# A decoder of four layers on one core: maxima over the partitions moved to GpSimd, the last context layer with one pass of scores, film and filter fused, and the bias copy moved forward

## The chip, the cores and the metric

The kernel runs on 1 core of one Trainium2 chip. The metric is the time of one execution on the device, in microseconds. Three runs of the kernel before gave 4775.98, 4770.83 and 4765.56 us, a median of 4770.83.

## What is computed

The input x has the shape (4, 256, 128): 4 batches of 256 positions with 128 channels. A context of shape (4, 1601, 96) serves four attention layers. The masks are all true. Twelve sublayers follow one another, each adding to x: self-attention, context attention and a feed-forward part for each of four layers. Those that the change touches are these.

Layer 0's context attention has 8 heads of 128. In the kernel all 1024 queries attend over all 4 x 1601 = 6404 context places, with a softmax:

```python
q, k, v = x_norm @ Wq, context @ Wk, context @ Wv
p = softmax(1.5 * scale * q @ k.T)
x = x + (p @ v) @ Wout + bout
```

Layer 1's context attention has 16 heads of 8. At its end a flag tells whether any score was not a number; then the mean of the values replaces the result.

Layer 2's context sublayer takes the best places of the context, and then steers the normalised input with the attended context c, filters it along time by a long convolution done as a Fourier transform, steers again, and ends with a Gelu network:

```python
scale, shift = split(gate * (c @ W_film + b_film))
y = y * (1 + scale) + shift
```

Layer 3's context sublayer quantises its tensors to 8-bit integers and its weights to three values, and adds two attentions in sequence to the fused text, each with one head of 64 over the 1601 places of the same batch:

```python
for i in range(2):
    q = fused folded to 64 columns
    fused = fused + 0.1 * twice(softmax(q @ keys_i.T * scale) @ values_i)
```

## The kernel before

The work is cut into stages. A stage (`Core.stage`, L72) is a block with one program for each engine, and all engines meet at its end. Within it the engines wait for each other on semaphores. SP issues the transfers. Five places matter.

**The first load.** `WeightsAhead.use` (L655) for the first layer lets SP issue, after the layer's own weights, the four copies of `ContextAhead.load` (L1258 to L1263): all weights of the heads (2048 KB), the context by columns (2401.5 KB), the context by rows (2448 KB, written in runs of 96 floats, 51 on each of 128 partitions) and the output bias (64 KB). The stage ends when SP is through with issuing. The data is waited for in `fold_weights` (L1223).

**Layer 0's context attention**, `attend_all_places` (L956). A unit is one head, one half of the queries (512) and one part of the 51 context tiles (24 or 27); there are 32 units. Groups of four tiles run through a ring of 11 buffers. The loop over steps s, written out by hand for each engine, does in each step: scores of group s on TensorE (L985), two copies to the ring on ScalarE (L1079), running maxima on VectorE (L1129), and for the group nine steps earlier the subtraction of the maximum (L1110), the exponential (L1065) and one step later the product with the context rows (L1010). The maximum over the partitions is made at a unit's end: VectorE folds to 128x512 (L1135, L1137), TensorE turns four tiles (L994), VectorE reduces (L1141), TensorE spreads the four columns out again (L1000), ScalarE copies them to `L0x_spread` (L1053). `turn` comes one step behind the unit's last group, `spread_out` two, `place` three.

**Layer 1's flag** (L1629 to L1659). VectorE reduces marks to one column (L1649), GpSimd takes the maximum over the partitions (L1642), VectorE widens it (L1651).

**Layer 2's film and filter**, `layer2_context` (L3581). After `best_places` come a stage that multiplies by the text mask (with its own 1 KB copy, L3599), a norm (`normalise`), a turn (`to_columns`), `linear_rows` with `modulate` (four small VectorE steps for each of 8 tiles, L3618 to L3621), a stage with the filter (L3634 forward, L3650 copies, L3653 to L3658 the products, L3641 back), `linear_rows` with `modulate` once more, and an addition (L3669). Then a norm with its turn, `linear_columns` (L316) and a stage that applies the Gelu (L1882).

**Layer 3's two attentions.** `project_image` (L3743) makes keys and values for both. Only 64 partitions hold keys; partition 64 is set to one by GpSimd (L3791). `attend_image` (L3794) is called twice. For each of 4 batches TensorE first makes the scores by queries (8 matmuls, `scan`, L3816), of which VectorE takes maxima (L3928, L3932). TensorE turns the negated maxima to a row (L3822), which ScalarE copies to the queries' partition 64 (L3890). So the second pass of scores (L3833, 13 tiles, K=65) comes out with the maximum already subtracted. ScalarE takes the exponential straight out of PSUM (L3898), TensorE multiplies with the values (L3844). The rest is the division (L3939 to L3947). The order of TensorE is written out by hand (L3855 to L3884).

On TensorE a matmul of f32 data is two instructions in the trace, a transposition is one.

## Time and profile before

| what | value |
|---|---|
| median of three runs | 4770.83 us |
| lowest and highest | 4765.56 and 4775.98 us |
| time of the profiled execution | 4773.13 us |
| its span | 4771.4 us |
| TensorE matmuls busy | 3660.8 us (77%) |
| VectorE busy | 3005.6 us (63%) |
| ScalarE busy | 1894.5 us (40%) |
| GpSimd busy | 260.7 us (5%) |
| mean granted clock of TensorE | 0.866 |

The profile is of one execution. Times are from the start of the span. PE is TensorE's matmuls, PEld its weight loads, which lie beside them; DVE is VectorE, ACT ScalarE, POOL GpSimd, SP the engine that issues transfers. L and a number is a line of the kernel. A row of the timeline gives the start, the time, the engine, the line, output and inputs, the count of instructions merged, and in brackets the idle time before and what ended it. The granted clock is 1.00 at 2.4 GHz and 0.50 at 1.2 GHz. The columns of the other views stand with their rows below.

### The profile page before, as it was taken

To read this page: it belongs to the slowest core of one execution; us is meant where nothing else is said; L and a number is where in the kernel's file an instruction comes from. 1 tells how busy PE (TensorE), PEld (TensorE's weight loads), DVE (VectorE), ACT (ScalarE), POOL (GpSimd) and SP (SyncE) were. 2 spreads that over 40 slices of the span, in tenths; PEclk is the share of its full clock that TensorE was granted. 3 is DMA by queue.
4 is the path that set the end of the run, shared out by engine and by line. 5 is a ranking of instruction groups with operands and counts; after the bars stand their busy time and mean duration, and the time that the engine had idled before them with its cause. 6 is when DMAs were issued, how large, how long until landed. Compare 5 with 4: busy or idle time off the path is not lost. (4 is left out here: it accounts for less than half of the span.)

```text
span 4771.4 us, 54706 instructions
## 1 busy us (share of the span) xinstructions
PE 3660.8 (77%) x21928; PEld 1970.9 (41%) x21928; DVE 3005.6 (63%) x4214; ACT 1894.5 (40%) x2113; POOL 260.7 (5%) x112
## 2 busy tenths in 40 slices
PE   4699999999999955577776772666544785879669
PEld 2434444444444423233336552332222464545356
DVE  3466666666666666589885437699985446442541
ACT  1255555555555532244441332244431343331123
POOL 0000000000000000000000000144430000000000
PEclk9799999999999977799997895666656986888789
DMA  2000000000000000100002001000001000000000
GB/s 74 8 0 0 1 0 0 0 1 0 0 1 0 1 11 12 20 8 7 8 1 85 27 2 38 0 0 0 0 0 37 2 36 8 36 1 0 1 10 32
DMA packets 12879, 55.80 MB, mean 12 GB/s; under 512 B 2209, under 2 KB 2721, under 8 KB 11970
## 3 DMA queue, kind: packets, MB, share of 16 engines
q1 hardware_dynamic: 12626, 52.31, 3.7%
q8 instruction: 174, 2.85, 0.2%
q14 instruction: 79, 0.65, 0.0%
HBM read 48.50 MB, written 0.52 MB: 10 GB/s over the span
## 5 line engine op out<-in xcount | busy, mean ns | idle before, releaser
L985 PE MATMUL banks<-L0x_q_context,L0x_context 96*128 96x512 f32 (+1 forms) x1632 | 742.0, 596 | 10.0 <-ACT L0x_ring L1079 9.3
L1010 PE MATMUL banks<-L0x_ring,L0x_context_rows 128*97 128x512 f32 (+1 forms) x1632 | 737.5, 594 | 1.1 <-ACT L0x_ring L1065 1.1
L1079 ACT COPY L0x_ring<-banks 128x1024 f32<-128x1024 f32 (+1 forms) x416 | 413.4, 996 | 657.8 <-PE banks L985 657.8
L1129 DVE TENSOR_TENSOR L0x_maxima<-L0x_maxima,L0x_ring 128x1024 f32<-128x1024 f32 (+1 forms) x288 | 342.6, 1194 | 257.2 <-ACT L0x_ring L1079 256.1
L1110 DVE TENSOR_TENSOR L0x_ring<-L0x_ring,L0x_spread 128x2048 f32<-128x2048 f32 (+1 forms) x208 | 457.2, 2200 | 18.4 <-ACT L0x_spread L1053 18.4
L985 PEld LDWEIGHTS banks<-L0x_q_context,L0x_context 96*128 96x128 f32 (+1 forms) x1632 | 300.1, 188 | 396.7 <-issue 378.0
L1010 PEld LDWEIGHTS banks<-L0x_ring,L0x_context_rows 128*97 128x97 f32 (+1 forms) x1632 | 262.0, 164 | 416.8 <-issue 413.6
L1065 ACT ACTIVATE L0x_ring<-L0x_ring 128x2048 f32<-128x2048 f32 (+1 forms) x208 | 384.4, 1849 | 11.4 <-DVE L0x_ring L1110 11.3
L1485 ACT ACTIVATE L1x_probs<-banks 128x2048 f32<-128x2048 f32 (+1 forms) x112 | 196.7, 1757 | 260.3 <-PE banks L1415 218.5
L1518 DVE TENSOR_REDUCE L1x_maxima<-banks 128x3 f32<-128x1203 f32 (+1 forms) x176 | 241.5, 1372 | 91.2 <-PE banks L1384 91.2
L1384 PE MATMUL banks<-L1x_k,L1x_q 32*128 32x401 f32 x1024 | 181.3, 591 | 120.3 <-DVE L1x_maxima L1518 104.8
L1541 DVE SCALAR_TENSOR_TENSOR L1x_probs<-L1x_probs,L1x_floor 128x1024 f32<-128x1024 f32 (+1 forms) x208 | 252.1, 1216 | 13.1 <-ACT L1x_probs L1485 13.1
L3262 PE MATMUL banks<-L2x_k,L2x_q_of_head 128*128 128x512 f32 (+1 forms) x256 | 183.8, 813 | 0.0
L3367 DVE MAX8 L2x_top<-L2x_rest 128x8 f32<-128x1601 f32 x96 | 175.5, 1828 | 3.3
L1415 PE MATMUL banks<-L1x_q_shifted,L1x_k 32*128 32x256 f32 (+1 forms) x1664 | 170.5, 398 | 5.3 <-ACT L1x_probs L1485 4.0
L3372 DVE MATCH_REPLACE8 L2x_rest<-L2x_top,L2x_rest 128x1601 f32<-128x1601 f32 x96 | 173.8, 1810 | 0.0
L243 PE MATMUL banks<-identity,z_rows 128*128 128x128 f32 x104 | 26.7, 437 | 170.9 <-DVE z_rows L276 170.9
L1384 PEld LDWEIGHTS banks<-L1x_k,L1x_q 32*128 32x128 f32 x1024 | 57.9, 196 | 209.2 <-DVE L1x_maxima L1518 180.9
L3335 POOL TENSOR_TENSOR L2x_exp_all<-L2x_exp_all,L2x_exp_rest 128x1601 f32<-128x1601 f32 x31 | 110.9, 3577 | 258.3 <-ACT L2x_exp_top L3325 258.3
L1415 PEld LDWEIGHTS banks<-L1x_q_shifted,L1x_k 32*128 32x128 f32 (+1 forms) x1664 | 108.4, 185 | 37.4 <-ACT L1x_probs L1485 14.6
L1429 PE MATMUL banks<-L1x_probs,L1x_v 128*16 128x256 f32 (+1 forms) x1664 | 115.9, 387 | 5.9 <-DVE L1x_probs L1541 4.2
L316 PE MATMUL banks<-z_columns,L_weights 128*128 128x512 f32 (+1 forms) x216 | 110.8, 675 | 11.2 <-PEq L77 11.2
(899 smaller groups left out, 5512.4 us busy)
## 6 DMA issues: line engine op xcount, KB each, us to landing
L1f_expert_weights<-in_L1f_experts SPq DMA_DIRECT2D x16, 512.0 KB, 10.9
L2f_expert_weights<-in_L2f_experts SPq DMA_DIRECT2D x8, 512.0 KB, 5.0
L3a_expert_weights<-in_L3a_experts SPq DMA_DIRECT2D x8, 512.0 KB, 5.1
L3f_expert_weights<-in_L3f_experts SPq DMA_DIRECT2D x8, 512.0 KB, 5.7
L1x_k<-L1x_k_rows SPq DMA_DIRECT2D x64, 50.0 KB
L0x_context_rows<-in_context_rows SPq DMA_DIRECT2D x1, 2448.0 KB, 27.8
L0x_context<-in_context SPq DMA_DIRECT2D x1, 2401.5 KB, 19.4
L1x_context<-in_context SPq DMA_DIRECT2D x4, 600.4 KB, 5.1
```

The lines of the kernel that those rows point to most:

```text
L985: mm = pe.matmul(k.ps[0:height(j), i, :], c1[:, j * P:j * P + height(j)], q1[:, u // 2 % 2, :], start=True, stop=True)
L1010: mm = pe.matmul(k.ps[0:CW, bank, :], rows1[0:height(j), j, :], ring[0:height(j), s % RING, i, :], start=s == FIRST[u] and i == 0, stop=s ...
L1065: ins = act.activation(ring[:, s % RING, 0:len(full), :], ring[:, s % RING, 0:len(full), :], ACT.Exp)
L1079: act.copy(ring[0:r, s % RING, 2 * p:2 * p + len(pair), :], k.ps[0:r, 2 * p:2 * p + len(pair), :]).then_inc(copied, 1)
L1110: ins = dve.tensor_tensor(o, o, spread_top[:, u % 2, None, :].broadcast_to([P, len(full), 512]), ALU.add)
L1129: dve.tensor_tensor(o, before, ring[0:r, s % RING, 2 * p:2 * p + m, :], ALU.max).then_inc(maxed, 1)
L1384: mm = pe.matmul(k.ps[:, i, 0:WIDE], qT[row(h), g, b * S + it * P:b * S + (it + 1) * P], kT[row(h), b % 2, g, 400 * c:400 * c + WIDE], sta ...
L1415: mm = pe.matmul(k.ps[0:height(j), 3 + h, i * S:(i + 1) * S], kT[row(h), b % 2, g, j * P:j * P + height(j)], qs[row(h), u % 2, :], start=T ...
L1485: act.activation(probs[0:r, at % 2, 0:m, :].rearrange("p a (h q) -> p h a q", h=4), k.ps[0:r, 3:7, 0:m * S].rearrange("p h (a q) -> p h a ...
L1518: dve.tensor_reduce(mx[:, u % 2, items[0]:items[-1] + 1], k.ps[:, 0:len(items), 0:WIDE], X, ALU.max).then_inc(reduced, 1)
L1541: dve.scalar_tensor_tensor(out=o, in0=o, scalar=1.0, in1=floor[0:height(j), u % 2, :], op0=ALU.min, op1=ALU.max).then_inc(clipped, 1)
L3262: mm = pe.matmul(k.ps[:, i, 0:m], qh[:, h, b * S + it * P:b * S + (it + 1) * P], kT[:, b % 2, c:c + m], start=False, stop=True)
```

## The change

Five edits, of which the first and third are small.

1. In `ContextAhead.load` the copy of the output bias is issued second, ahead of the context by columns and by rows.
2. In `attend_all_places` the two sets of transposes, VectorE's reduction and ScalarE's copy are replaced by one `partition_all_reduce` of 128x512 on GpSimd, whose result lies on all partitions (`L0x_greatest`). It has the other sign, so the additions become subtractions. For odd units VectorE takes the maximum with the even unit's result before.
3. In layer 1 the flag is summed over the partitions by a matmul with ones in place of GpSimd's maximum.
4. In layer 2 `steer` holds mask, norm, turn, both films' matmuls and the first film in one stage, and `filter_long` the filter and the second film. The gate is multiplied to weights and biases ahead; sums and products go over wide tiles. The mask's copy goes with those of `filter_spectrum`. `gelu_columns` applies the Gelu to PSUM, in the stage of the matmuls.
5. In layer 3 `attend_image` has one pass of scores. Keys and queries lie twice, on partitions 0 to 63 and 64 to 127, and tiles of one group take them in turn. ScalarE copies the scores to a ring of three batches (the third lies in `L3x_big`), VectorE takes the maxima over tiles, GpSimd over partitions, VectorE subtracts, ScalarE takes the exponential in place. The scores run two batches ahead of the values.

The core of the diff:

```diff
 # ContextAhead.load
         sp.dma_start(self.heads[:], k.dram["L0x_heads"]).then_inc(self.here, 16)
+        sp.dma_start(self.bout[:], k.dram["L0_xattn_rows"].broadcast_to([P, P])).then_inc(self.here, 16)
         sp.dma_start(self.c1[:].rearrange("c (b n) -> c b n", b=B), k.dram["context"].rearrange("b c n -> c b n")).then_inc(self.here, 16)
         sp.dma_start(self.rows1[:, :, 0:CD], k.dram["context_rows"]).then_inc(self.here, 16)
-        sp.dma_start(self.bout[:], k.dram["L0_xattn_rows"].broadcast_to([P, P])).then_inc(self.here, 16)

 # attend_all_places
-            def turn(u):
...
-            def spread_out(u):
...
-            def place(u):
...
-            def greatest(u):
...
+                if u:
+                    dve.wait_ge(placed, u)
+                ins = dve.tensor_tensor(folded_top[:], top[:, 0, 0, :], top[:, 0, 1, :], ALU.max)
                 if u % 2:
+                    ins.then_inc(joined, 1)
+                    dve.wait_ge(joined, u // 2 + 1)
+                    ins = dve.tensor_tensor(folded_top[:], folded_top[:], greatest[:, 0, :], ALU.max)
+                ins.then_inc(folded, 1)
...
+        @block.gpsimd
+        def _(pool):
+            for u in range(UNITS):
+                pool.wait_ge(folded, u + 1)
+                if u >= 2:
+                    pool.wait_ge(shifted, LAST[u - 2] + 1)
+                    pool.wait_ge(differed, u // 2)
+                pool.partition_all_reduce(greatest[:, u % 2, :], folded_top[:], P, RMAX).then_inc(placed, 1)

 # layer1_context
+                pe.wait_ge(counted, 1)
+                pe.matmul(k.ps[:, 1, 0:1], k.ones[:], flag[:, 0:1], start=True, stop=True).then_inc(everywhere, 1)
                 pe.wait_ge(widened, 1)
...
-                pool.partition_all_reduce(flag[:, 1:2], flag[:, 0:1], P, RMAX).then_inc(everywhere, 1)
...
+                step(dve.tensor_copy(flag[:, 1:2], k.ps[:, 1, 0:1]))

 # steer: the VectorE part
+                dve.tensor_tensor(ct[:], ct[:], mask[:, :, None].broadcast_to([P, TILES, P]), ALU.mult).then_inc(masked, 1)
+                for n in names:
+                    dve.tensor_scalar(w[n], w[n], w["gate"], None, ALU.mult).then_inc(gated, 1)
+                for i, n in enumerate(names):
+                    step.start(dve.tensor_scalar(shift[:, i, :], w["b_" + n], w["gate"], None, ALU.mult))
+                step.settle()
+                step(dve.tensor_scalar(shift[:, :, 0:P], shift[:, :, 0:P], 1.0, None, ALU.add))
...
+                for p in range(4):
+                    dve.wait_ge(product, p + 1)
+                    step.start(dve.tensor_tensor(film[:, 0, 2 * p:2 * p + 2, :], k.ps[:, 2 + p, :].rearrange("p (t n) -> p t n", t=2),
+                                                 shift[:, 0, None, :].broadcast_to([P, 2, 2 * P]), ALU.add))
+                step.settle()
+                step(dve.tensor_tensor(xin[:], xin[:], film[:, 0, :, 0:P], ALU.mult))
+                dve.tensor_tensor(xin[:], xin[:], film[:, 0, :, P:2 * P], ALU.add)

 # filter_long: the VectorE part
+                for f in range(2):
+                    dve.wait_ge(spectral, f + 1)
...
+                    step.start(dve.tensor_tensor(ys[:, 0, f], real, kc, ALU.mult))
+                    step.start(dve.tensor_tensor(tmp[:, 0], imag, ks, ALU.mult))
+                    step.start(dve.tensor_tensor(ys[:, 1, f], real, ks, ALU.mult))
+                    step.start(dve.tensor_tensor(tmp[:, 1], imag, kc, ALU.mult))
+                    step.settle()
+                    step.start(dve.tensor_tensor(ys[:, 0, f], ys[:, 0, f], tmp[:, 0], ALU.subtract))
+                    step(dve.tensor_tensor(ys[:, 1, f], ys[:, 1, f], tmp[:, 1], ALU.add))
+                    dve.sem_inc(ready, 1)
...
+                for i in range(TPB):
+                    dve.wait_ge(back, i + 1)
+                    step(dve.tensor_tensor(times[:, i], times[:, i], k.ps[:, i, :].rearrange("p (b d) -> p b d", b=B), ALU.add))
+                    step(dve.tensor_tensor(times[:, i], times[:, i], scales[:, i], ALU.mult))
+                    step(dve.tensor_tensor(times[:, i], times[:, i], shifts[:, i], ALU.add))
+                    dve.tensor_tensor(outs[:, i], times[:, i], rows[:, i], ALU.add)

 # attend_image: TensorE's scores and order
+                for i, j in enumerate(groups[g]):
+                    r, t = min(P, CTX - j * P), slice(64 * (i % 2), 64 * (i % 2) + 64)
+                    mm = pe.matmul(k.ps[0:r, 2 * (n % 2) + i % 2, (i // 2) * S:(i // 2 + 1) * S], keys[t, b, j * P:j * P + r],
+                                   q1[t, b * S:(b + 1) * S], start=True, stop=True)
...
+            for b in range(B):
+                for g in range(G):
+                    if b + 2 < B:
+                        score(b + 2, g)
+                    add(b, g)
+                    if g == 1 and b:
+                        set_upright(b - 1)
 # attend_image: ScalarE's order
+            for b in range(B):
+                for g in range(G):
+                    exponentials(b, g)
+                    if b + 2 < B:
+                        take(b + 2, g)
+                keep(b)
 # attend_image: VectorE's order
+            maximum(0)
             for b in range(B):
                 if b + 1 < B:
+                    maximum(b + 1)
+                shift(b)
+                if b >= 2:
+                    finish(b - 2)
+            finish(B - 2)
             finish(B - 1)
+
+        @block.gpsimd
+        def _(pool):
+            for b in range(B):
+                pool.wait_ge(folded, b + 1)
+                if b >= 2:
+                    pool.wait_ge(shifted, G * (b - 1))
+                pool.partition_all_reduce(greatest[:, b % 2, :], folded_top[:], P, RMAX).then_inc(placed, 1)
```

## Rows read from the trace of the kernel before

**Rows 1.** The page: the span, and TensorE's busy time, share and instructions.
```profile
span 4771.4 us, 54706 instructions
PE 3660.8 (77%) x21928; PEld 1970.9 (41%) x21928; DVE 3005.6 (63%) x4214; ACT 1894.5 (40%) x2113; POOL 260.7 (5%) x112
```

**Rows 2.** Busy time in stretches: stretch, length, engines busy (instructions), granted clock, DMA share, GB/s.
```profile
300.00:1600.00 1300.00, 1300.00 (x3341) 550.99 (x3340) 879.45 (x714) 716.66 (x618) 0.00 (x0) 1.00 0.00 0
2100.00:2300.00 200.00, 153.88 (x1740) 77.27 (x1734) 181.45 (x164) 90.68 (x100) 0.00 (x0) 0.99 0.05 9
3150.00:3500.00 350.00, 218.79 (x532) 93.56 (x531) 338.65 (x340) 161.03 (x170) 147.09 (x44) 0.63 0.00 0
4271.40:4360.50 89.10, 85.36 (x300) 48.79 (x300) 22.04 (x52) 19.23 (x27) 0.00 (x0) 0.90 0.00 1
4363.00:4452.50 89.50, 86.14 (x300) 50.10 (x300) 21.79 (x51) 17.94 (x26) 0.00 (x0) 0.89 0.00 1
```

**Rows 3.** Timeline of the start, and one later issue of SP's.
```profile
14.01 0.68 SPq L1262 DMA_DIRECT2D L0x_context_rows<-in_context_rows  x1
14.73 24.20 SPq L1263 DMA_DIRECT2D L0x_output_bias<-in_L_xattn_rows  x1
39.41 1.64 DVE L181 BATCH_NORM_STATS2 norm_stats<-x_residual 128x6 f32<-128x128 f32 x8 [26.52 <-PEq L77]
...
3679.92 0.51 SPq L637 DMA_DIRECT2D L_weights<-in_L_attn_rows  x1
```

**Rows 4.** Timeline of layer 0's context attention around the end of one unit.
```profile
1037.35 0.69 DVE L1137 TENSOR_TENSOR L0x_folded_maxima<-L0x_maxima 128x512 f32<-128x512 f32 x1
...
1044.42 0.60 PE L994 MATMUL banks<-identity,L0x_folded_maxima 128*128 128x128 f32 x4
1044.86 3.60 PE L985 MATMUL banks<-L0x_q_context,L0x_context 96*128 96x512 f32 x8
...
1048.30 0.60 PE L1000 MATMUL banks<-identity,L0x_minus_max 128*128 128x128 f32 x4
...
1048.73 3.60 PE L1010 MATMUL banks<-L0x_ring,L0x_context_rows 128*97 128x512 f32 x8
...
1051.83 2.29 DVE L1110 TENSOR_TENSOR L0x_ring<-L0x_ring,L0x_spread 128x2048 f32<-128x2048 f32 x1 [1.06 <-ACT L0x_spread L1053]
```

**Rows 5.** GpSimd's reductions by line, and the timeline of the flag.
```profile
L3714 POOL PARTITION_ALL_REDUCE L3x_scales<-L3x_scales x3 | 1.1, 351 | 230.4 <-DVEq L3724 230.4
L2353 POOL PARTITION_ALL_REDUCE L3x_magnitude<-L3x_magnitude x1 | 0.5, 490 | 5.9 <-DVE L3x_magnitude L2298 5.9
...
2513.38 0.38 POOL L1642 PARTITION_ALL_REDUCE L1x_flag<-L1x_flag x1 [595.66 <-issue]
2513.79 0.69 DVE L1651 CAST L1x_probs<-L1x_flag 128x1024 int32<-128x1024 f32 x1 [5.63 <-POOL L1x_flag L1642]
```

**Rows 6.** Timeline of layer 2's film, filter and Gelu network.
```profile
3563.07 1.23 DVE L3605 TENSOR_TENSOR L2x_rows<-L2x_rows,L2x_text_bytes 128x1024 f32<-128x1024 f32 x1 [2.00 <-DMA L2x_text_bytes<-in_text_mask]
...
3590.33 9.90 PE L3634 MATMUL banks<-L2x_rows,L_weights 128*128 128x512 f32 x16 [7.21 <-PEq L77]
...
3596.91 0.69 DVE L3650 COPY L2x_spectra<-banks 128x512 f32<-128x512 f32 x1 [2.10 <-PE banks L3634]
...
3634.58 1.64 DVE L264 BATCH_NORM_STATS2 norm_stats<-L2x_rows 128x6 f32<-128x128 f32 x8 [0.30 <-PEq L77]
...
3642.10 9.62 PE L316 MATMUL banks<-z_columns,L_weights 128*128 128x512 f32 x16 [1.15 <-PEq L77]
...
3657.92 8.77 PE L357 MATMUL banks<-L_weights,L2x_hidden 128*128 128x128 f32 x64 [6.20 <-PEq L77]
```

**Rows 7.** Timeline of the first `attend_image`; then a group by line and shape, whole span.
```profile
4352.49 1.89 PE L3833 MATMUL banks<-L3x_q,L3x_k 65*128 65x256 f32 x8
...
L1415 PE MATMUL banks<-L1x_q_shifted,L1x_k 32*128 32x256 f32 x1536 | 154.0, 398 | 5.0 <-ACT L1x_probs L1485 3.8 <-ACT L1x_floor L1480 1.2
```

**Rows 8.** Group by line and shape in the first `attend_image`: busy us, mean ns, idle before.
```profile
L3898 ACT ACTIVATE L3x_probs<-banks 128x1024 f32<-128x1024 f32 x12 | 12.3, 1025 | 34.1 <-PE banks L3833 34.1
```

412 lines of the change are left out of this document (194 added, 218 removed).

## The prediction

> **What bounds the kernel now.** I read the page's share of engines first, then busy time in stretches, then for each edit the timeline of its stage. TensorE is busy 77% of the span [rows 1], but the stages have different limits. From 300 to 1600 us (layer 0's context attention) TensorE is busy for all 1300 us at a granted clock of 1.00, VectorE for 879 and ScalarE for 717: there only TensorE's work counts. Both calls of `attend_image` are TensorE's as well (85.4 of 89.1 us, 86.1 of 89.5), at a mean clock of 0.90 and 0.89 [rows 2]. At the start, in layer 1's flag and in layer 2's film the bound is a chain, and the reader is to follow hand-over after hand-over. The sum is made against the profiled execution (4773.13 us, 2.3 above the median of the runs, 4770.83). A measurement tells about 0.2%, some 10 us, from no change.
>
> **1. Bias copy second instead of last.** SP issues the context rows in 0.68 us, then holds 24.20 us in the issue of the small bias copy behind them; VectorE's first real work starts at 39.41, 0.48 us after SP is free [rows 3]. With the bias second, the big copy is SP's last, and nothing is queued behind it: four issues from 13.15, at 0.33, 0.43, 0.43 and 0.68 with gaps, end near 15.2, and the stage near 15.7. Who needs the data waits at 208 us. That a short copy passes behind large ones still in flight shows at 3679.92: the fifth issue in a row took 0.51 us [rows 3]. So it is the 6528 short runs of the rows copy, and not the number of copies, that held SP. Gain 23.5 us; bounds 0 (the big copy itself waits) and 24.
>
> **2. Layer 0's context attention.** Per unit (32 of them) TensorE loses two sets of four transposes. In place they take 1044.42 to 1044.86 and 1048.30 to 1048.73, so 0.44 + 0.43 = 0.87 us [rows 4]; 32 x 0.87 = 27.9 us, all on the bound. VectorE loses 32 reductions of 0.69 and 16 of 0.16 (24.7 us) and gains 16 maxima of 0.69 (11.0): nothing, since it is busy 68%. ScalarE loses 32 copies of 0.58: nothing, busy 55%.
> The new step is GpSimd's reduction of 128x512 over the partitions. No row has this width: 1 column took 0.35 us and 7 columns 0.49 [rows 5]. 6 columns for 0.14 us make 0.0233 each, so 0.35 + 511 x 0.0233 = 12.3 us on that slope. Bounds: 0.49 if the width costs nothing more, 512 x 0.35 = 179 if every column costs like the first. The kinds differ (maximum, sum), and GpSimd's spans are rough. I take 11, near the slope, since it is the only one there is. What covers it: the folded maxima are done at 1038.04 and the first subtraction that needs them started at 1051.83, 13.8 us later, behind a place in VectorE's order that the edit does not move [rows 4]. Behind that subtraction stands an exponential of 1.9 us, and its product comes only in TensorE's next step, 6.9 us on: by estimate a further 4.9 us of slack. Up to 18.7 us TensorE feels nothing; in units of six groups there is a step of 6.9 us more. Two places have no such cover: the last unit, where everything drains (11 against the 9 us that transposes and copy took), and the first use. At 2513.38 the first reduction in the program started 5.2 us after its input was there [rows 5], the later ones at once; that first use moves here. Together -1.5. Gain 26.4 us.
> Beside this row stands a page. The Trainium skill (GPSIMD Engine Reference, 3.2) gives 247,699 ns for GpSimd's `tensor_reduce` along the partitions at 128x2048; as an estimate from that page 62 us for 512 columns. It is another instruction than this one. By the rows the sum is the 26.4 above, by the page's rate the stage would lose 1275 us (worked out under the rivals); the row of 7 columns speaks against that rate.
>
> **3. Layer 1's flag.** VectorE waits 5.63 us for GpSimd, from 2508.16 to 2513.79 [rows 5]. A one-column product and a copy out of PSUM (0.25 + 0.15, with hand-overs 0.6) take its place; the four products now behind it are done before the mask is written (0.69). Gain 5.0 us; bounds 4.5 and 5.3.
>
> **4. Layer 2's film and filter.** Before, from the mask's wait at 3561.1 to the statistics at 3634.58: 73.5 us [rows 6]. After, on VectorE, `steer`: mask 1.23; gates and biases five times 0.35 to 0.39, 1.9; statistics to root 3.9; eight scalings 2.2; gain and shift 2.5; four additions of 128x512 at 0.72, 2.9; product and sum 2.5. That makes 17.1, with 0.7 of borders 17.8 (28.7 before). TensorE's 16 matmuls of the first film lie beside the norm, the 16 of the second as well. `filter_long`: eight matmuls, of which the first run at the low clock (6.6 us, as the second copy out of PSUM was reached at 3596.91 from 3590.33 [rows 6]), then twice six VectorE steps of 0.73, 8.8; D_skip 1.26 beside the way back; way back 3.6 after the last product; two tails of four steps, 5.8; borders 0.5. That makes 25.3 to 26.5, where 44.8 stood. The 64 small film steps of 0.29 to 0.42, the four copies out of PSUM and the stage of the last addition are gone. Gain 73.5 - 17.8 - 26.2 = 29.5 us; bounds 26 (TensorE at the low clock all along) and 32.
> Gelu out of PSUM: from 3642.10 to 3657.92 there are 9.6 us of TensorE, then a table load and a pass over 4096 columns in a stage of its own [rows 6]. Afterwards the last 128x512 Gelu (0.69) ends the stage: 9.6 + 0.7 + 0.6 = 10.9. Gain 4.9 us. The mask's 1 KB copy rides among the spectrum's, which wait for 20 us of context anyway: nothing.
>
> **5. `attend_image`, twice.** TensorE loses per batch the scan (six matmuls of 512, two of 65) and a turn. The scores (26 instructions of 256 columns at 0.216, 5.6 us; eight take 1.89 with 0.38 for the last one's end [rows 7]) go on two row tiles: four row tiles ran at 154.0/1536 = 0.100 a piece [rows 7], so I take a factor of 1.7 (bounds 1 and 2), 3.3 us. With the values (5.6) and the turn 9.2 us a batch at full clock, 18 at half. VectorE per batch: maxima 1.22, 1.22, 0.42, 0.69, 0.42; subtractions 3 x 1.22 + 0.42; finish 0.95; hand-overs 0.6: 9.6. ScalarE: 2 x (3 x 1.02 + 0.38) + 0.37 = 7.3 [rows 8]. GpSimd: 256 columns, 0.35 + 255 x 0.0233 = 6.3, or half of 11, 5.7.
> Each engine waits for the others in a fixed order, so I stepped through it. Shift of batch 0 starts at 16.0 us: query 1.7, scores and copies of two groups, maxima, reduction 5.7, second fold. From a shift to the next 12.7: subtraction 1.2, exponential 1.2, two values and two scores in turn on TensorE 5.5, copy 1.2, maxima to fold 3.6. The fourth shift comes 6.0 after the third, the end 12.3 later: 16.0 + 25.4 + 6.0 + 12.3 = 59.7 us at full clock. At half clock the same steps give 92. TensorE has more gaps than now. Where it was busy 77% of a stretch the clock was 0.99; where 63%, 0.63 [rows 2]. In the new order it is busy 64% at full clock. I take the low level for the first 30 us of a call: 69.5. Gain 178.6 - 139.0 = 39.6 us. The key memset of 10.8 us on GpSimd goes, but ended before its stage did: nothing.
>
> **Sum.** 23.5 + 26.4 + 5.0 + 29.5 + 4.9 + 39.6 = 128.9. 4773.1 - 128.9 = 4644.2, less 2.3 for the median: 4642 us.
>
> **Rivals.**
> *The clock stays low in `attend_image`.* 94 us a call in place of 69.5: 4691 us. For it: the 0.63 at a like share of TensorE [rows 2]. Against: at the low clock TensorE would itself be 83% busy, and such stretches were granted more. Chance 0.13.
> *The start gives nothing*: SP hangs in the rows copy itself, or the transfer that now runs beside layer 0 delays it. 4642 + 23.5 = 4665 us. Against: 0.68 us behind the same copies in rows 3. Chance 0.11.
> *GpSimd's reduction breaks its cover: slower.* It decides from 18.7 us for 512 columns. At 30 us a unit of seven groups stalls TensorE 11.3 and one of six 4.4: 16 x 15.7 = 251 us. `attend_image` at 15 us stands at 86 a call, 33 more: 4642 + 251 + 33 = 4926 us. It meets no change near 26 us. For it: VectorE works 68% of the time beside it, and the one slope is from 7 columns. Against: that slope gives 12.3. Chance 0.06.
> *Every column costs like the first*, 0.35 us: 179 us for 512. 16 x (160.3 + 153.4) = 5019 us in layer 0; in layer 3 four reductions of 90 and some 25 around them, 385 a call, 631 more: 10292 us. The 0.49 of 7 columns speaks against it. Chance 0.02. Between this and the forecast lies the rate that the Trainium skill (GPSIMD Engine Reference, 3.2) has for `tensor_reduce`: by its 62 us 16 x (43.3 + 36.4) = 1275 us, and at 31 us and 147 a call 155 in layer 3, an estimate from that page of 6072 us.
> *Cheaper still*: reduction of 5 us and `attend_image` at 58 to 60 us a call, 4642 - 20 - 4 = 4618 us. Chance 0.15.
> Forecast itself 0.53, for 4625 to 4660.
>
> **Numbers.** 4642 us. The range reaches over the clock and start rivals to 4700 and down to 4612; it leaves out the two slow reductions and some of the cheap end. Faster 0.91, same 0.01, slower 0.08, which is the two reductions.
>
> **What would show it.** VectorE's first statistics near 16 us; TensorE still busy all of layer 0's attention, some 27 us shorter, its reduction under 13 us and no wait of the subtractions for it over 2 us outside the first and last unit; 44 to 45 us between mask and statistics in layer 2; each `attend_image` near 70 us with the clock low only at its start. Wrong it would be if TensorE showed idle time in layer 0 once a unit, or if SP's rows issue took over 20 us.

## The result and the profile after

The changed kernel takes 4625.43 us in the median of 4 runs (4621.06 to 4626.79), where the kernel before took 4768.87 beside it. The ratio is 0.9696 with a 95% interval of 0.9679 to 0.9713. The profiled executions are 147.3 us apart (spans 4771.4 and 4624.1). The prediction was 4642 us with a range of 4612 to 4700, and faster at 0.91. It was right, with a gain some 15 us larger than forecast (143.4 us between the medians, 128.9 forecast).

The page of the changed kernel, span and engines' busy time, against [rows 1]:

```profile
span 4624.1 us, 53788 instructions
PE 3545.3 (77%) x21514; PEld 1886.8 (41%) x21514; DVE 3007.0 (65%) x4129; ACT 1899.2 (41%) x2110; POOL 390.9 (8%) x150
```

TensorE lost 115 us of work and stayed at 77% of the span. GpSimd gained 130 us of work, which the span does not show.

To see where the time went I cut each trace at nine places, always at the start of the same instruction: VectorE's first statistics, the first scores of layer 0's context attention, its last reciprocal, layer 1's flag, layer 2's mask multiplication, the product behind the Gelu, the first query product of the first attention of layer 3 and the last of its second one, and the first write of `L3x_joined`. The lengths between them, in us (each is a difference of two starts in the timelines; the gain at the flag lies in the stretch from the flag to layer 2's mask):

```
stretch                         before   after   difference
start to first statistics         39.4    16.1     23.3
to layer 0's attention           187.2   182.4      4.8
layer 0's attention             1500.1  1474.6     25.5
to layer 1's flag                781.2   782.1     -0.9
flag to layer 2's mask          1055.2  1050.6      4.6
mask to the Gelu's product        94.8    56.8     38.0
to the first attention           613.8   609.2      4.6
first attention, with turn        92.9    70.7     22.2
second attention, with turn       95.3    69.9     25.4
rest                             311.5   311.7     -0.2
```

**The start.** All four copies are issued in a row, and the stage's end follows at once (SPq is SyncE's queue; the columns are those of [rows 3]):

```profile
13.61 0.43 SPq L1239 DMA_DIRECT2D L0x_output_bias<-in_L_xattn_rows  x1
14.56 0.83 SPq L1241 DMA_DIRECT2D L0x_context_rows<-in_context_rows  x1
16.07 1.65 DVE L181 BATCH_NORM_STATS2 norm_stats<-x_residual 128x6 f32<-128x128 f32 x8 [3.09 <-PEq L77]
```

The big copy alone holds SyncE for 0.83 us, where the small one behind it had held it for 24.20 [rows 3].

**Layer 0's attention.** From 300 to 1600 us TensorE is still busy throughout; below it stand the two calls of `attend_image` (busy time in stretches, columns of [rows 2]):

```profile
300.00:1600.00 1300.00, 1300.00 (x3174) 538.68 (x3173) 889.75 (x700) 716.34 (x602) 117.84 (x29) 1.00 0.00 0
4171.50:4236.60 65.10, 49.13 (x220) 27.28 (x220) 36.07 (x53) 30.06 (x39) 7.00 (x4) 0.87 0.00 1
4239.50:4304.70 65.20, 49.37 (x220) 27.38 (x220) 36.01 (x53) 28.77 (x38) 6.97 (x4) 0.87 0.00 1
```

The timeline of a unit's end, and GpSimd's step as a group of the page:

```profile
1038.56 0.69 DVE L1113 TENSOR_TENSOR L0x_folded_maxima<-L0x_maxima 128x512 f32<-128x512 f32 x1
...
1039.34 4.35 POOL L1182 PARTITION_ALL_REDUCE L0x_greatest<-L0x_folded_maxima  x1 [37.27 <-DVE L0x_folded_maxima L1113]
1039.77 2.28 DVE L1082 TENSOR_TENSOR L0x_ring<-L0x_ring,L0x_greatest 128x2048 f32<-128x2048 f32 x1
...
1051.78 1.22 DVE L1082 TENSOR_TENSOR L0x_ring<-L0x_ring,L0x_greatest 128x1024 f32<-128x1024 f32 x1
...
L1182 POOL PARTITION_ALL_REDUCE L0x_greatest<-L0x_folded_maxima x32 | 127.1, 3973 | 1476.4 <-DVE L0x_folded_maxima L1113 759.5
```

The reduction of 128x512 takes 3.97 us in the mean. This one is over at 1043.69, 8 us before the first subtraction that needs it (1051.78). In [rows 4] that place held transposes, a reduction and a copy of three engines.

**Layer 1's flag.** The copy that widens the flag starts 0.66 us after the end of VectorE's reduction (2455.52), where it took 5.63 [rows 5]:

```profile
2455.25 0.27 DVE L1623 TENSOR_REDUCE L1x_flag<-L1x_nans 128x1 f32<-128x112 f32 x1
2455.57 0.38 PE L1612 MATMUL banks<-L1x_flag,ones 128*128 128x1 f32 x2 [2.12 <-DVE L1x_flag L1623]
...
2456.18 0.69 DVE L1626 CAST L1x_probs<-L1x_flag 128x1024 int32<-128x1024 f32 x1
```

**Layer 2.** The timeline of film, filter and Gelu, answering to [rows 6]:

```profile
3505.83 1.23 DVE L3594 TENSOR_TENSOR L2x_rows<-L2x_rows,L2x_text_bytes 128x1024 f32<-128x1024 f32 x1 [0.32 <-PEq L77]
...
3522.31 9.24 PE L3646 MATMUL banks<-L2x_rows,L_weights 128*128 128x512 f32 x16 [6.63 <-PEq L77]
3528.16 0.69 DVE L3672 TENSOR_TENSOR L2x_products<-banks,L2x_spectrum 128x512 f32<-128x512 f32 x1 [3.36 <-PE banks L3646]
...
3538.24 0.69 DVE L3685 TENSOR_TENSOR L2x_rows<-L2x_rows,banks 128x512 f32<-128x512 f32 x1 [0.86 <-PE banks L3655]
...
3544.19 1.64 DVE L264 BATCH_NORM_STATS2 norm_stats<-L2x_rows 128x6 f32<-128x128 f32 x8 [0.30 <-PEq L77]
...
3551.73 9.89 PE L3700 MATMUL banks<-z_columns,L_weights 128*128 128x512 f32 x16 [1.15 <-PEq L77]
3562.64 0.57 PE L357 MATMUL banks<-L_weights,L2x_hidden 128*128 128x128 f32 x3 [1.02 <-PEq L77]
```

From the mask's wait (3505.51, against 3561.07 before) to the statistics it is 38.7 us where it was 73.5; the 2.0 us of waiting for the mask's copy are gone, and the 0.3 that are left are the stage's border. From the first matmul to the product behind the Gelu it is 10.9 us instead of 15.8.

**Layer 3.** The second `attend_image`, its scores, GpSimd's steps and VectorE's subtractions, all from the timeline:

```profile
4239.81 3.75 PE L3900 MATMUL banks<-z_columns,L3x_both_halves 128*128 128x512 f32 x4 [1.03 <-PEq L77]
...
4251.04 1.06 POOL L4015 PARTITION_ALL_REDUCE L3x_greatest_score<-L3x_folded_top  x1 [31.45 <-DVE L3x_folded_top L3974]
...
4252.66 1.14 PE L3876 MATMUL banks<-L3x_q,L3x_k 64*128 64x256 f32 x8 [0.74 <-ACT L3x_ring L3929]
...
4255.69 4.24 DVE L3980 TENSOR_TENSOR L3x_ring<-L3x_ring,L3x_greatest_score 128x1024 f32<-128x1024 f32 x4
4255.87 1.97 POOL L4015 PARTITION_ALL_REDUCE L3x_greatest_score<-L3x_folded_top  x1 [3.76 <-DVE L3x_folded_top L3974]
...
4271.18 4.24 DVE L3980 TENSOR_TENSOR L3x_ring<-L3x_ring,L3x_greatest_score 128x1024 f32<-128x1024 f32 x4
...
4285.64 4.24 DVE L3980 TENSOR_TENSOR L3x_big<-L3x_big,L3x_greatest_score 128x1024 f32<-128x1024 f32 x4
...
4290.73 3.82 DVE L3980 TENSOR_TENSOR L3x_ring<-L3x_ring,L3x_greatest_score 128x1024 f32<-128x1024 f32 x4
```

The four subtractions start 15.5, 14.5 and 5.1 us after one another. GpSimd's maximum for batch 1 is there at 4257.84, yet the subtraction of batch 1 starts only at 4271.18: the maximum of batch 2 stands ahead of it in VectorE's order. The first subtraction is held in the same way: its maximum is there at 4252.10, and it starts at 4255.69 behind the maximum of batch 1.

### The profile page after: what moved, and what is told of

Its sections match the earlier page's. It is cut to its first block and busy times, and to the rows that moved or that the text cites. A ratio compares the mean times of both kernels' runs of the same rounds, so it can differ in the third digit from the quotient of the medians.

```text
span 4624.1 us, 53788 instructions
## 1 busy us (share of the span) xinstructions
PE 3545.3 (77%) x21514; PEld 1886.8 (41%) x21514; DVE 3007.0 (65%) x4129; ACT 1899.2 (41%) x2110; POOL 390.9 (8%) x150
## 5 line engine op out<-in xcount | busy, mean ns | idle before, releaser
L996 PE MATMUL banks<-L0x_ring,L0x_context_rows 128*97 128x512 f32 (+1 forms) x1632 | 737.1, 594 | 1.8 <-ACT L0x_ring L1040 1.8
L1082 DVE TENSOR_TENSOR L0x_ring<-L0x_ring,L0x_greatest 128x2048 f32<-128x2048 f32 (+1 forms) x208 | 458.2, 2205 | 45.9 <-ACT L0x_ring L1054 45.9
L1182 POOL PARTITION_ALL_REDUCE L0x_greatest<-L0x_folded_maxima x32 | 127.1, 3973 | 1476.4 <-DVE L0x_folded_maxima L1113 759.5
L1103 DVE TENSOR_TENSOR L0x_maxima<-L0x_ring 128x1024 f32<-128x1024 f32 x64 | 78.4, 1225 | 118.5 <-ACT L0x_ring L1054 118.5
## 6 DMA issues: line engine op xcount, KB each, us to landing
L0x_context<-in_context SPq DMA_DIRECT2D x1, 2401.5 KB, 20.6
```

Of the source, the lines that this page charges most:

```text
L996: mm = pe.matmul(k.ps[0:CW, bank, :], rows1[0:height(j), j, :], ring[0:height(j), s % RING, i, :], start=s == FIRST[u] and i == 0, stop=s ...
L1082: ins = dve.tensor_tensor(o, o, greatest[:, u % 2, None, :].broadcast_to([P, len(full), 512]), ALU.subtract)
L1103: dve.tensor_tensor(o, before, ring[0:r, s % RING, 2 * p:2 * p + m, :], ALU.max).then_inc(maxed, 1)
```

## Experiments

**One edit alone, four times.** Each kernel is the one before with a single edit. First the bias copy:

```diff
         sp.dma_start(self.heads[:], k.dram["L0x_heads"]).then_inc(self.here, 16)
+        sp.dma_start(self.bout[:], ...).then_inc(self.here, 16)
...
-        sp.dma_start(self.bout[:], ...).then_inc(self.here, 16)
```

> The kernel before with the bias copy second and nothing else. Theory A, each edit's gain is its own: VectorE's first statistics start near 16 us instead of 39.4 and the whole gets 23.3 us shorter (4745 from 4769). Theory B, the start interacts with what follows: in the changed kernel layer 0's context attention began 28.1 us earlier (195.8 against 223.9), though only 23.3 of it lie before the first statistics; the other 4.8 come from a higher granted clock between them (0.90 against 0.85 over that stretch). If that belongs to the earlier start, it is here too and the gain is about 28 us; if it varies from run to run, the stretch from the first statistics to the attention differs from 184.5 us by some other amount.

Then GpSimd's maxima in layer 0 (edit 2 whole, nothing else):

```diff
-            def turn(u):
...
+                pool.partition_all_reduce(greatest[:, u % 2, :], folded_top[:], P, RMAX).then_inc(placed, 1)
```

> The kernel before with only layer 0's maxima on GpSimd. Theory A: TensorE loses 32 x 0.87 us of transposes and the stage is 25 to 27 us shorter, as in the changed kernel (1503.2 to 1477.6 us); the whole 4743. Rival: some of the 25.5 us came from elsewhere (the earlier start, or the context rows landing at another time), and alone the stage gains under 20 us.

Then layer 2 (edit 4 whole):

```diff
+            steer(k, w, mask, ct, z0, xin, film, shift)
+            filter_long(k, w, spectrum, xin, z0, film, shift, xt)
...
+            gelu_columns(k, h, w["w1"], w["b1"])
```

> The kernel before with only layer 2's film, filter and Gelu rewritten. Theory A: from the end of the choice of places to the statistics 38.7 us instead of 73.5, and 4.9 us in the Gelu; the whole 40 us shorter, 4729. Rival: 3 to 5 us of that belong to a clock that stands high there only in the changed kernel (0.91 in its trace from 3505 to 3544 us), and alone the stretch takes 42 us or more.

Then layer 3 (edit 5 whole):

```diff
+                pool.partition_all_reduce(greatest[:, b % 2, :], folded_top[:], P, RMAX).then_inc(placed, 1)
...
-            pool.memset(keys[64:65], 1.0)
```

> The kernel before with only layer 3's attention changed. Theory A: each call takes 65.2 us against 89.1 and 89.5, the two with the turn between them 48 us shorter, the whole 4721. Rival: the clock in these calls depends on what ran before them; alone a call is 3 us or more off 65.2.

The flag (edit 3) was not run alone.

Measured, against 4775.75 us of the kernel before on the same chip: bias 4757.82 (ratio 0.9957, 0.9943 to 0.9972), reduction 4738.21 (0.992, 0.9905 to 0.9935), film 4733.11 (0.991, 0.9896 to 0.9925), attention 4725.87 (0.9893, 0.9876 to 0.9909). Each is under 2%, and no interval reaches 1. The stretches, cut at the same instructions as above:

```
                           before  bias  reduction  film   image  after
start to first statistics    39.4   16.2      39.2   39.9   39.2   16.1
to layer 0's attention      187.2  186.3     182.3  186.0  182.0  182.4
layer 0's attention        1500.1 1500.1    1474.6 1500.2 1502.9 1474.6
flag to layer 2's mask     1055.2 1062.5    1048.8 1050.7 1061.5 1050.6
mask to Gelu's product       94.8   94.7      94.7   56.6   95.1   56.8
first attention, turn        92.9   92.9      93.0   93.0   71.3   70.7
second attention, turn       95.3   95.3      95.3   95.2   70.2   69.9
```

Each edit changes its own stretch by what it changed in the full version, to within 0.6 us: in their stretches these four edits add up, and theory A holds. The whole times came within 5 us of those expected, except for the bias: 4757.8 instead of 4745. What does not belong to any edit are the second line and a part of the fourth. The stretch ahead of layer 0's attention took 187.2 us before and 182.0 with only the last layer changed, so its 4.8 us are not the earlier start's.

The flag-to-mask stretch took 1055.2, 1062.5 and 1061.5 us in three kernels that are alike there. With the reduction alone it took 1048.8, and 5 of those us have a cause. This kernel still has GpSimd's maximum at the flag:

```profile
2478.34 0.27 DVE L1626 TENSOR_REDUCE L1x_flag<-L1x_nans 128x1 f32<-128x112 f32 x1
2478.71 0.39 POOL L1619 PARTITION_ALL_REDUCE L1x_flag<-L1x_flag  x1 [593.38 <-DVE L1x_flag L1626]
2479.12 0.69 DVE L1628 CAST L1x_probs<-L1x_flag 128x1024 int32<-128x1024 f32 x1 [0.51 <-POOL L1x_flag L1619]
```

VectorE waits 0.51 us for it, where it waited 5.63 before, 5.57 with the bias alone, 5.51 with the film alone and 5.62 with the attention alone. In those four the flag's reduction is the program's first; here and in the changed kernel the first one stands in layer 0. So edit 2 by itself already removes what was forecast as edit 3's gain, and beside edit 2 the matmul of edit 3 (0.66) is worth nothing. Nor does layer 0 pay for being first: in the changed kernel the fold ends at 233.94 and the reduction starts at 234.08. Why the 5 us don't move there stays open.

The rest is spread. The rows of that stretch, for the bias alone and the reduction alone:

```profile
2486.90:3549.40 1062.50, 644.53 (x4866) 391.19 (x4866) 761.51 (x1065) 366.85 (x461) 219.13 (x72) 0.70 0.05 17
```
```profile
2478.30:3527.10 1048.80, 636.49 (x4866) 384.72 (x4866) 761.15 (x1066) 366.82 (x461) 219.04 (x72) 0.71 0.05 17
```

Of the 13.7 us between them 5.1 are the flag. VectorE's and ScalarE's busy times agree to 0.4 us. TensorE's is 8.0 us apart for the same 4866 instructions, at a granted clock of 0.70 and 0.71, so what varies besides is its clock. That, and the flag, is why the bias alone gained 17.9 us by the medians and 23.2 in its own stretch, and the reduction 37.5 and 25.5. Layer 0's attention varies as well: 1502.9 us with only the last layer changed.

**How far layer 0's reduction is covered.** The reduction of every unit is done n times, one waiting for the other:

```diff
+                for _ in range(3):
+                    step(pool.partition_all_reduce(greatest[:, u % 2, :], folded_top[:], P, RMAX))
                 pool.partition_all_reduce(greatest[:, u % 2, :], folded_top[:], P, RMAX).then_inc(placed, 1)
```

Four times:

> The changed kernel with each of layer 0's 32 reductions over the partitions done four times, one after the other (the same result is written four times). Their mean in the changed kernel is 3.97 us, so the step takes about 16 us. Theory A, the cover is 18.7 us (13.8 up to the first subtraction and 4.9 behind it): TensorE stays busy without a gap, the stage takes 1478 to 1484 us (the last unit alone pays 12 us, in full view), the whole 4636 to 4640 against 4625. Rival, the cover ends where the first subtraction used to start: from 13.8 us on each unit loses the difference, 2 us or more in each of 16 units of seven groups, 35 us or more besides the last unit's 12.

Six times (`range(5)`):

> The changed kernel with each of layer 0's reductions done six times, about 24 us. Theory A, cover 18.7 us and 6.9 more in units of six groups: 16 units lose 24 - 18.7 = 5.3 us each, 85 us, the last one 20 in full view, the stage near 1580 us. Rival, cover 13.8 us: 10 us in each of 16 units and 3 in the others, over 210 us. A third way is that the step is not six times as long because the mean of 3.97 us holds contention with VectorE, which would show in the durations first.

Ten times (`range(9)`):

> The changed kernel with each of layer 0's reductions done ten times. Four took 11.3 us together and six 15.1 us, 1.9 us for each further one, so ten take about 23 us. Theory A, the cover is 18.7 us in units of seven groups and 25.6 in units of six: 16 units lose 23 - 18.7 = 4.3 us of TensorE each, 69 us, the last unit another 17: the stage about 1560 us where it was 1474.6. Rival 1, the cover ends at 15 us, just behind what six reductions took: 8 us in 16 units and 1 in the others, over 160 us with the last. Rival 2, the cover is over 23 us: only the last unit's 17 us.

Measured: 4632.49 us with four (ratio to before 0.97, 0.9684 to 0.9716), and in one run each 4635.39 with six and 4746.58 with ten. The stage took 1479.1, 1484.0 and 1593.9 us against 1474.6. With four and six TensorE has all 1300 us of 300 to 1600 busy as before, and the rest falls to the last unit. Four took 11.3 us together, not 16, so that run can't tell a cover of 13.8 us from one of 18.7. Six took 15.1 us, not 24 (the third way of that expectation, taken up below): no stall at 15.1 refutes the cover of 13.8. Ten show where the cover ends (timeline of one unit, then TensorE's waits over the stage: us in total, times, longest):

```profile
1059.93 0.69 DVE L1117 TENSOR_TENSOR L0x_folded_maxima<-L0x_folded_maxima,L0x_greatest 128x512 f32<-128x512 f32 x1
...
1081.68 1.78 POOL L1185 PARTITION_ALL_REDUCE L0x_greatest<-L0x_folded_maxima  x1
1083.50 2.29 DVE L1082 TENSOR_TENSOR L0x_ring<-L0x_ring,L0x_greatest 128x2048 f32<-128x2048 f32 x1 [11.06 <-POOL L0x_greatest L1185]
...
1087.79 5.11 PE L996 MATMUL banks<-L0x_ring,L0x_context_rows 128*97 128x512 f32 x8 [4.18 <-ACT L0x_ring L1040]
...
PE banks L996 <- ACT L0x_ring L1040: 84.1, 18, 14.9
```

From the fold's end (1060.62) to the last reduction's (1083.46) it is 22.8 us, and TensorE waits 4.18: the cover is 18.7 us. The waits come to 84.1 us where the changed kernel has 1.8, against 86 expected. The stage lost 119: of the other 37 us 36 are TensorE's own work, since line 996 is busy 773.1 us in place of 737.1. The eight matmuls behind the stall took 5.11 us instead of 3.60, and the granted clock there was 0.69 (1087 to 1092.5 us). The stall of 4.2 us cost a further 1.5 in clock.

**What the reduction costs.** Three stages that only measure are put ahead of layer 3's attention; they add time:

```diff
+            for n in (1, 7, 64, 128, 256, 512, 1024, 2048):
+                for _ in range(2):
+                    step(pool.partition_all_reduce(target[:, 0:n], source[:, 0:n], P, RMAX))
...
+                for n in (128, 256, 512, 1024):
+                    for _ in range(2):
+                        step(pool.partition_all_reduce(target[:, 0:n], source[:, 0:n], P, RMAX))
```

> The changed kernel with three stages added ahead of layer 3's attention that do no work of the kernel's: reductions over the partitions of 1, 7, 64, 128, 256, 512, 1024 and 2048 columns, twice each, alone; then 128, 256, 512 and 1024 beside VectorE in 1024-column maxima back to back; then the same beside ScalarE in 1024-column copies. Theory A, the step costs a base and a small rate by width, and what stretched it was VectorE: from 1.06 us for 256 columns and 1.78 for 512 the rate is 2.8 ns a column and the base 0.34, so 128 columns take 0.70, 1024 take 3.2 and 2048 take 6.1; beside VectorE each waits for the maximum in progress (1.2 us), beside ScalarE nothing is added. Theory B, the first-to-last spread of 1.8 to 4.35 us belongs to the step itself (a fixed alternation or the state of its code): then it shows alone too, and ScalarE or VectorE beside it make no difference.

Measured alone, for 1, 7, 256, 512, 1024 and 2048 columns (timeline of GpSimd, one of each pair; 64 and 128 columns took 0.55 and 0.70):

```profile
4173.39 0.35 POOL L4035 PARTITION_ALL_REDUCE L3x_ring<-L3x_ring  x1 [10.33 <-DVE L3x_ring L4026]
4174.28 0.40 POOL L4035 PARTITION_ALL_REDUCE L3x_ring<-L3x_ring  x1
...
4178.11 1.06 POOL L4035 PARTITION_ALL_REDUCE L3x_ring<-L3x_ring  x1
4180.42 1.78 POOL L4035 PARTITION_ALL_REDUCE L3x_ring<-L3x_ring  x1
4184.17 3.23 POOL L4035 PARTITION_ALL_REDUCE L3x_ring<-L3x_ring  x1
4190.81 6.11 POOL L4035 PARTITION_ALL_REDUCE L3x_ring<-L3x_ring  x1
```

From 256 columns on that is 0.34 us and 2.8 ns a column. Beside ScalarE's copies the same widths took 0.70, 1.06, 1.78 and 3.22 us, no more. Beside VectorE's maxima (which read two tensors in SBUF) 128 columns took 1.57 and 1.25 us, 256 took 1.61 and 1.46, 512 took 2.18 and 1.89, 1024 took 3.33 and 4.00. Theory A holds in its widths and in naming VectorE; the addition, 0.1 to 0.9 us, is less than a whole maximum each time. VectorE pays as well, and more for a wider reduction: its maxima took 1.23 us with no reduction beside them, 1.52 beside 256 columns, 1.94 beside 512 and 2.80 beside 1024. The widest pair:

```profile
4214.34 3.33 POOL L4045 PARTITION_ALL_REDUCE L3x_ring<-L3x_ring  x1
4214.61 2.80 DVE L4052 TENSOR_TENSOR L3x_big<-L3x_big 128x1024 f32<-128x1024 f32 x1
```

The 4.35 us in layer 0 fit 1.78 of work and some 2.3 of being held off by the subtraction of 2.28 us beside it.

**GpSimd in layer 3.** Each of the four reductions of a call done three times:

```diff
+                for _ in range(2):
+                    step(pool.partition_all_reduce(greatest[:, b % 2, :], folded_top[:], P, RMAX))
```

> The changed kernel with each of layer 3's four reductions per call done three times. Theory A, GpSimd is not on the chain of attend_image: what holds VectorE's subtraction of batch b is the maximum of batch b + 1, which stands ahead of it and waits for ScalarE's copies; a call gets longer by 2 us at most, at its first batch. Rival, the reduction is on the chain of every batch: 2 x 2 us by 4 batches, 14 to 16 us a call, the whole near 4655 us.

Measured: 4621.92 us in one run, the attentions with their turns 69.0 and 69.7 us against 70.7 and 69.9. Three reductions of a batch take 5 us in place of 2 and nothing moves. GpSimd is not on that chain.

**VectorE's order in layer 3.**

```diff
-            maximum(0)
-            for b in range(B):
-                if b + 1 < B:
-                    maximum(b + 1)
-                shift(b)
+            maximum(0)
+            maximum(1)
+            shift(0)
+            for b in range(B):
+                if b + 1 < B:
+                    shift(b + 1)
+                if b + 2 < B:
+                    maximum(b + 2)
```

> The changed kernel with VectorE's order altered in attend_image: the subtraction of batch b + 1 stands ahead of the maximum of batch b + 2 instead of behind it. Theory A, the order of VectorE sets the 15 us from one subtraction to the next: copies of batch b + 2, its maximum, then only the subtraction of b + 1, whose maximum over the partitions had been there for 10 us. With the order altered the exponentials never wait, a batch takes the 9 to 10 us of TensorE's and ScalarE's work, and a call 53 to 57 us instead of 65.2; the whole 4601 to 4609. Rival, the pace comes from TensorE's clock: fewer gaps but the same mean, and a call stays at 62 to 65 us. A reduction then stands between each maximum and its subtraction, but off the chain.

Measured: 4616.15 us (4608.55 to 4618.14), ratio to before 0.9662 (0.9648 to 0.9677). The attentions with their turns take 66.5 and 62.8 us, 4.2 and 7.1 less. Batches 0 and 1 are now subtracted in one go, the next two at 4269.34 and 4279.84:

```profile
4253.91 7.98 DVE L3980 TENSOR_TENSOR L3x_ring<-L3x_ring,L3x_greatest_score 128x1024 f32<-128x1024 f32 x8
...
4269.34 3.83 DVE L3980 TENSOR_TENSOR L3x_big<-L3x_big,L3x_greatest_score 128x1024 f32<-128x1024 f32 x4 [1.19 <-POOL L3x_greatest_score L4018]
...
4279.84 3.83 DVE L3980 TENSOR_TENSOR L3x_ring<-L3x_ring,L3x_greatest_score 128x1024 f32<-128x1024 f32 x4 [1.19 <-POOL L3x_greatest_score L4018]
```

The middle batches now take 10.5 us (exponentials at 4266.99 and 4277.49), so the order was what held them at 15. The expectation of 53 to 57 us a call was too good: the first took some 61 us, and the second, from 4237.58 to 4296.25, 58.7, of which 16.3 lie ahead of the first subtraction and 16.4 behind the last; only the middle shrank. Part of the second call's 7.1 us is clock: it ran at 0.93 in the mean instead of 0.87, and TensorE was busy 45.5 us instead of 49.4. The first, which gained 4.2, ran at 0.89. This version beats both kernels: its two stretches are 11.3 us shorter, its median 9.3; the 2 us between lie in stretches that it leaves alone.

**One row tile.** The scores all on partitions 0 to 63:

```diff
-                    r, t = min(P, CTX - j * P), slice(64 * (i % 2), 64 * (i % 2) + 64)
+                    r, t = min(P, CTX - j * P), slice(0, 64)
```

> The changed kernel with attend_image's scores all on partitions 0 to 63, one row tile in place of two. Eight score instructions took 1.14 us and sixteen 2.00 on two row tiles, 0.108 each; on one they should take 0.216 each, so 26 x 0.108 = 2.8 us more of TensorE a batch. Theory A, the scores of batch b + 2 stand between the values of batch b on TensorE and are on the chain: a call gets 8 to 11 us longer at full clock, less what a busier TensorE gains in granted clock. Rival, TensorE has gaps enough (49 of 65 us busy) and a call gets longer by under 3 us.

Measured: 4658.62 us in one run; the attentions with their turns 89.1 and 84.8 us, 18.4 and 14.9 more. Theory A holds in kind and is too small in size. The scores are busy 75.2 us over both calls in place of 33.9, twice 20.6 more, where 11 a call were worked out at full clock: the clock adds to them instead of giving back. Three stretches follow. The first two are from the second call, where both first batches are scored on one tile and on two. The third is from the first call on one tile, with the scores of its second batch:

```profile
4260.97:4284.20 23.23, 22.92 (x53) 16.60 (x52) 5.22 (x6) 6.71 (x8) 1.06 (x1) 0.50 0.00 0
```
```profile
4243.48:4252.66 9.18, 7.24 (x53) 4.71 (x53) 5.39 (x6) 6.78 (x9) 1.06 (x1) 1.00 0.00 0
```
```profile
4181.00:4196.00 15.00, 14.66 (x34) 10.56 (x34) 7.16 (x10) 5.23 (x7) 1.48 (x2) 0.50 0.00 0
```

Just before that, from 4175 to 4181, the first batch was scored on one tile at a granted clock of 1.00.

**What held SyncE at the start.**

```diff
+        sp.dma_start(self.rows1[:, :, 0:CD], k.dram["context_rows"]).then_inc(self.here, 16)
         sp.dma_start(self.bout[:], ...).then_inc(self.here, 16)
         sp.dma_start(self.c1[:]..., k.dram["context"]...).then_inc(self.here, 16)
-        sp.dma_start(self.rows1[:, :, 0:CD], k.dram["context_rows"]).then_inc(self.here, 16)
```

> The changed kernel with the four copies of the first load in the order heads, rows of the context, bias, columns of the context. Theory A, what held SyncE for 24.2 us in the kernel before is the copy in 6528 short runs that stood ahead: the bias issue behind it now takes over 20 us, and the first statistics start 23 us later than in the changed kernel, near 39 us. Rival, it was the count: any fourth copy behind three large ones waits; then the bias is issued in under 1 us and the columns' copy, the fourth now, is what takes over 20 us.

Measured: 4636.00 us in one run. The timeline, and from the pages how long the rows copy took from its issue to landing, first in the kernel before, then in this one:

```profile
13.57 0.68 SPq L1239 DMA_DIRECT2D L0x_context_rows<-in_context_rows  x1
14.30 12.66 SPq L1240 DMA_DIRECT2D L0x_output_bias<-in_L_xattn_rows  x1
27.01 0.43 SPq L1241 DMA_DIRECT2D L0x_context<-in_context  x1
```
```profile
L0x_context_rows<-in_context_rows SPq DMA_DIRECT2D x1, 2448.0 KB, 27.8
```
```profile
L0x_context_rows<-in_context_rows SPq DMA_DIRECT2D x1, 2448.0 KB, 16.3
```

The issue that waits is the one right behind the rows copy, third or fourth; the fourth, of 2401.5 KB, takes 0.43 us. That speaks for theory A's cause. Its length was wrong: 12.66 us, not over 20, and the first statistics start at 27.9. The 2401.5 KB no longer lie ahead of the rows copy, which so lands earlier. In both orders the hold ends 2.9 us before the rows copy has landed (38.93 against 41.8 us, 26.96 against 29.9). So it lasts nearly as long as that copy is in flight; that the short runs, and not the 2448 KB, make it so was not separated.

## Why the prediction was right, point by point

1. *The start.* 23.5 us forecast, 23.3 measured. The rows copy as the cause stands up to the changed order; that it is its short runs is not shown by itself. The rival "the start gives nothing" is refuted: the rows copy itself took 0.83 us to issue.
2. *Layer 0.* 26.4 forecast, 25.5 measured, alone as well as with the rest. The transposes were put at 27.9 (32 times 0.87 is 27.8) and 1.5 taken off for the first use and the last unit. Neither cost shows: the first reduction starts 0.14 us after its input, and the last is over at 1637.27, while VectorE is subtracting for the unit before until 1638.67. So 25.5 stands against 27.8, and that the total fits so well is in part luck. The cover of 18.7 us was worked out from one timeline, and the tenfold reduction gave 18.7. The step's price was mis-sized: 11 us taken, 3.97 measured in place and 1.78 alone. The slope between 1 and 7 columns came from two reductions of different kinds (0.35 and 0.49 us); by itself the step costs 0.40 for 7 columns, and from 256 on a column costs 2.8 ns where the slope had 23.3. The Trainium skill (GPSIMD Engine Reference, 3.2), whose figure for `tensor_reduce` gave 62 us in the prediction, doesn't carry over to this instruction: the 128x2048 for which it has 247,699 ns took 6.11 us here. Both slow rivals are refuted.
3. *The flag.* 5.0 forecast; the hand-over went from 5.63 to 0.66 us, 4.97. The size was right and the credit wrong: with the reduction alone the same hand-over took 0.51 us, so edit 2 had removed the 5 us already. The prediction did say that the first use moves to layer 0, and charged it there.
4. *Layer 2.* 29.5 and 4.9 forecast, 34.8 and 4.9 measured. The mechanism was right and the terms too large. From the stage's start to that of the filter it is 16.8 us with its border, where 17.8 stood. In `filter_long`, where 26.2 stood, 21.9 were measured (3522.31 to 3544.19): the forward matmuls gave the first product after 5.85 us, not 6.6, and twice six products took 8.0, not 8.8, since steps that don't wait for one another started every 0.60 us here. The way back held VectorE only 2.1 us (3536.15 to 3538.24), not 3.6, because the first half of the rows can be finished while TensorE makes the second.
5. *`attend_image`.* 39.6 forecast, 47.6 measured. The first subtraction came 15.9 us after the start (16.0 forecast), which is luck: 5.7 us of the 16.0 were the reduction, and the trace has the maximum of batch 1 on that chain instead. The intervals 15.5, 14.5 and 5.1 add up to 35.0, where 12.7, 12.7 and 6.0 make 31.4; the end took 14.0, not 12.3. The step that failed is the one on the clock: 9.8 us a call were set aside for 30 us at the low level. The clock was low for the first 4 us (0.51), 1.00 for the next 9 and 0.87 in the mean, 65.2 us in all. The steps at full clock were put at 59.7, too short by 5.5, so two errors partly cancel and the forecast of 69.5 is 4.3 too long. How much of the 5.5 is clock and how much order was not separated. Two terms were too dear and did not matter: the reduction (5.7 us taken, 1.06 to 1.97 measured) is off the chain, and the row tiles gave a factor of 2.0 (16 scores take 2.00 us and eight 1.14, so eight more take 0.86, 0.108 each, against 0.216), not 1.7. What paces the middle batches, VectorE's own order, was in the steps that gave 12.7 but not named.

The terms as measured make 23.3 + 25.5 + 5.0 + 34.8 + 4.9 + 47.6 = 141.1 us. The other 6.2 of 147.3 are not the edits' by any run here: 4.8 ahead of layer 0's attention, which took 182.0 to 187.2 us in kernels that are alike there, 4.6 between the Gelu's product and layer 3's attention, where the other kernels with edits 4 and 5 took up to 3.2 us longer than the changed one, and together -3.2 elsewhere.

## What to carry to other kernels

Moving a step to an idle engine is safe when the cover is counted in the trace, hand-over by hand-over, up to where the bound engine would feel it; here the price was off by a factor of three and the forecast held, because the cover was counted correctly. Before an edit is given credit for a wait, ask whether another edit removes it too: a single run would have shown that the flag's 5 us went with the first reduction. Where several small edits go together, cut both traces at the same instructions: stretches agree to a few tenths where whole runs differ by ten microseconds through the clock. A long stretch of middling load does not agree so well (1055.2 to 1062.5 us here). Ahead of an ordered engine, put first what is already ready: VectorE held a subtraction for 13 us behind a maximum whose input was late, and turning the two round gave 11 us more.

## What the runs showed of the hardware that was not expected

GpSimd and VectorE hold each other off. A reduction of 1.78 us took 4.35 when VectorE's subtraction of 2.28 us began beside it, and in the kernel with six reductions a subtraction of 2.28 us became 3.14 beside them. ScalarE's copies did neither. The Trainium skill (SBUF — State Buffer, "SBUF: two separate sides") says that the two engines share a pair of ports under an exclusive lock, taken for a whole instruction, when VectorE reads two tensors from SBUF beside a GpSimd instruction that reads SBUF. The 4.35 agree with that in size. In two ways the traces do not: that reduction had begun 0.43 us before the subtraction, which still took its usual 2.28, and a maximum of 2.80 us began and ended inside a reduction of 3.33 us that was only 0.1 longer than alone. So here neither instruction kept the other out from its start to its end.

The granted clock fell while TensorE was busy. With the scores of the first call on one row tile it was 1.00 until 4181 and 0.50 (1.2 GHz) for the next 15 us, of which TensorE was busy 14.7; in the second call it was 0.50 already and stayed so for 23.2 us, busy 22.9. On two row tiles it was 1.00 (2.4 GHz) at 7.2 of 9.2 us, and in layer 0, with matmuls of 96 and 128 rows, 1.00 while TensorE was busy for 1300 of 1300. So busy time alone does not say which level is granted; whether it is the half of the rows that lies idle was not tried further.

The first reduction over the partitions started 5.2 us after its input when it stood at layer 1's flag (2508.16 to 2513.38), and 0.14 us after it when it stood in layer 0 (233.94 to 234.08). The one at the flag then started 0.10 us after its own.

A small copy's issue can hold SyncE until shortly before the transfer ahead of it lands: 24.20 and 12.66 us behind a copy in 6528 short runs, each time up to 2.9 us before its landing, and 0.43 us in front of it.
